# Routing in two groups with fixed 2048-row regions for each expert, and a tail summed on TensorE

## What is computed

```
x = x + align(ctx, layernorm(x))       # per batch b: ctx (77, 128)
x = x + ffn(layernorm(x))

align: D = pairwise distances (77 x 512); R = dynamic time warping cost of D
       walk back from the last cell to (0, 0); expanded[j] += ctx[i] on each cell of the path

ffn(xf), xf of shape (2048, 128), E = 8 experts, 2 chosen for each token:
       scores = sigmoid(xf @ gate_w + bias); the two largest, divided by their sum, are the weights w
       eo[e]  = gelu(xf @ up_w[e] + up_b[e]) @ down_w[e] + down_b[e]      # 128 -> 512 -> 128
       out    = 0.1 * sum over chosen e of w[e] * eo[e]  +  0.1 * (the shared expert, same form)
       out    = out / (max |out| over the row + 1e-6)
```

## Time and profile before

| | us |
|---|---|
| median of 3 runs | 290.02 |
| lowest, highest | 288.14, 290.07 |
| the profiled execution | 287.41 |
| its span (first to last instruction) | 285.7 |
| busy: PE, DVE, ACT, POOL | 161.6, 193.9, 128.6, 112.5 |

### The profile page before, as it was taken

How to read it: one execution, slowest core, us unless ns; L and a number is a source line. 1 busy time by engine, 2 the same in 40 slices (tenths; PEclk the granted TensorE clock), 3 DMA queues, 4 the chain that set the end, 5 groups by cost and what they waited for, 6 DMA issues and landing times. The chain is left out here.

```text
span 285.7 us, 5134 instructions
## 1 busy us (share of the span) xinstructions
PE 161.6 (57%) x1262; PEld 108.3 (38%) x1263; DVE 193.9 (68%) x926; ACT 128.6 (45%) x323; POOL 112.5 (39%) x210
## 2 busy tenths in 40 slices
PE   1690089991000014663478995099999999982000
PEld 0330034430000013642322331069999999972000
DVE  3843999999955816856539690058888888860590
ACT  5550049950003032295076421058888888850020
POOL 8100030000000023030477777325888888874540
PEclk9997559998555555555579999559999999999555
DMA  7013999994330000000011111222333323101922
GB/s 202 2 40 83 134 317 331 204 181 69 65 61 7 1 0 2 2 1 0 20 56 49 47 47 55 66 58 78 92 84 91 92 77 98 39 3 27 267 73 73
DMA packets 39747, 22.83 MB, mean 80 GB/s; under 512 B 14796, under 2 KB 36787, under 8 KB 39719
## 3 DMA queue, kind: packets, MB, share of 16 engines
q1 hardware_dynamic: 36824, 17.98, 27.3%
q0 software_dynamic: 2496, 4.24, 4.5%
q10 hardware_dynamic: 399, 0.28, 0.3%
HBM read 12.51 MB, written 10.89 MB: 82 GB/s over the span
## 5 line engine op out<-in xcount | busy, mean ns | idle before, releaser
L646 POOL DMA_INDIRECT expert_dram<-arena_d,result_place x46 | 47.8, 1039 | 14.7 <-issue 12.1
L793 ACT ACTIVATE arena_f<-bank,tile_bias 128x256 f32<-128x256 f32 x92 | 36.3, 474 | 3.4 <-PE bank L939 2.6
L937 PE MATMUL bank<-down_hi,arena_d 128*128 x184 | 32.8, 220 | 1.0 <-DVE arena_g L1302 1.0
L938 PE MATMUL bank<-arena_a,up_hi 128*128 128x256 f16 (+1 forms) x108 | 33.1, 307 | 0.0
L1302 DVE TENSOR_TENSOR arena_g<-arena_f,arena_d 128x512 f16<-128x512 f32 x46 | 31.8, 692 | 1.6
L939 PE MATMUL bank<-down_hi,arena_g 128*128 x184 | 32.6, 219 | 0.0
L938 PE MATMUL bank<-down_lo,arena_d 128*128 x184 | 32.6, 219 | 0.0
L605 POOL COPY met_at<-arena_b 32x3 f16 (+1 forms) x26 | 3.9, 181 | 67.6 <-DVE arena_b L1145 63.4
L1085 DVE TENSOR_TENSOR_SCAN arena_b<-arena_c,edge,arena_a 64x33 f32<-64x33 f32 x92 | 25.6, 278 | 4.7 <-DMA arena_a<-dist_dram 4.6
L884 PE MATMUL bank<-arena_b,minus_one 128*128 (+1 forms) x26 | 3.9, 185 | 43.1 <-issue 43.1
L937 PE MATMUL bank<-arena_d,up_hi 128*128 128x256 f16 x92 | 26.1, 284 | 0.5 <-DVE arena_a L1294 0.5
(11 more groups left out here) (232 smaller groups left out, 443.5 us busy)
## 6 DMA issues: line engine op xcount, KB each, us to landing
sorted_dram<-padding SPq DMA_DIRECT2D x1, 2990.0 KB, 20.6
arena_g<-sorted_dram SPq DMA_DIRECT2D x23, 130.0 KB, 2.1
arena_d<-in_L_ffn_up_w SPq DMA_DIRECT2D x6, 256.0 KB, 4.7
arena_d<-in_L_ffn_down_w SPq DMA_DIRECT2D x5, 256.0 KB, 5.2
x_sb<-in_x SPq DMA_DIRECT2D x4, 256.0 KB, 4.4
arena_b<-expert_dram SPq DMA_DIRECT2D x4, 256.0 KB, 4.0
arena_c<-expert_dram SPq DMA_DIRECT2D x4, 256.0 KB, 4.4
out<-x_sb SPq DMA_DIRECT2D x4, 256.0 KB, 2.3
```

The source lines that it names most:

```text
L646: pool.indirect_dma_start(out=expert_dram.ap(), in_=y_row[:, j % Y_SLOTS, n, :], in_offset=None, out_offset=bass.IndirectOffsetOnAxis(ap=p ...
L793: last = act.activation(hid[:, k, m, cols], banks[UP_BANK + HALVES * k + m][:, cols], ACT.Gelu, bias=bias, scale=1.0 / WSCALE)
L937: pe.matmul(o, a_hi, b_hi, start=start, stop=False)
L938: pe.matmul(o, a_hi, b_lo, start=False, stop=False)
```

## The change

Each expert gets a region of its own of 2048 rows in `sorted_dram`, which grows from 23 x 256 to 8 x 2048 + 256 = 16,640 rows. A row's place then depends on its expert and its rank alone, not on the counts of the other experts. So routing is done in two groups (`ROUTED`): batch 0 first (4 tiles), then the other 12. The places of the second group start behind the first's counts (`first_row`). GpSimd scatters batch 0's rows for both choices (8 DMAs), copies y of batch 3 for the second choice, and scatters the rest (24). VectorE's, ScalarE's and TensorE's calls are put in an order of their own for this: batch 0's logits, choice and places come before the low halves of the batches 1 to 3.

Because tiles are no longer contiguous, the first row of each of the 23 tiles is computed (`tile_row`; unused tiles point to a pad tile), and SP reads it into a register ahead of each load. The padding is written by ScalarE's queue in the loop of the weight split (at n == 2), from a source of 13 rows on each partition that lies in `x2`.

The gates are turned once, in one transpose of 128x128, and their product with the biases, laid out block by block in `bias_of_tile` (VectorE clears it, SP loads 16 small blocks during the experts), is now done in the tail. The shared expert's bias is added by ScalarE as it keeps `accT`. The shared expert uses banks 0 to 3, for which all four sums have to be copied out first (`keep_sum`).

In the tail, ScalarE's queue reads the second choices and SP's the first. TensorE sums everything in PSUM: gates times biases, `accT` times the identity (instead of the transposes), and both results times the identity. VectorE finds the peak in PSUM, ScalarE scales all four tiles of a batch, VectorE adds the residual for the batch in one operation. GpSimd has no part in it, and each batch has an output buffer of its own.

```diff
+CAPACITY = B * S
+PAD_ROW = E * CAPACITY
+FILL_ROWS = 13
+ROUTED = (0, TPB), (TPB, TILES)
...
-        sorted_dram = nc.dram_tensor("sorted_dram", (EXPERT_TILES * ET, H + 2), F32, kind="Internal")
+        sorted_dram = nc.dram_tensor("sorted_dram", (PAD_ROW + ET, H + 2), F32, kind="Internal")
...
-        S_DOWN_BANKS = 7, 5
-        S_UP_BANKS = 6, 3
+        S_DOWN_BANKS = 2, 3
+        S_UP_BANKS = 0, 1
+        GATES_BANK = 4
+        RANK_BANKS = 4, 5
...
             def load(j, k):
-                rows = sorted_dram.ap()[j * ET:(j + 1) * ET, :].rearrange("(p n) d -> p n d", n=PARTS)
-                sp.dma_start(x_row[:, k], rows).then_inc(x_row_in[k], 16)
-
+                first = sp.value_load(tile_row[0:1, j:j + 1], min_val=0, max_val=PAD_ROW)
+                sp.dma_start(x_row[:, k], sorted_dram.ap()[bass.ds(first, ET), :].rearrange("(p n) d -> p n d", n=PARTS)
+                             ).then_inc(x_row_in[k], 16)
+
+            sp.wait_ge(table_ready, 2)
             sp.wait_ge(scattered, 16 * TOP * TILES)
             for k in range(SLOTS):
                 load(k, k)
@@ -513,21 +526,18 @@
                 sp.wait_ge(xT_in_psum, j - SLOTS + 1)
                 sp.wait_ge(place_kept, j - SLOTS + 1)
                 load(j, j % SLOTS)
+                if j == SLOTS:
+                    sp.wait_ge(bias_cleared, 1)
+                if j < SLOTS + TILES:
+                    t = j - SLOTS
+                    sp.dma_start(bias_of_tile[t * E:(t + 1) * E, t * H:(t + 1) * H], down_b).then_inc(bias_in, 16)
...
+            read_results(sp, 0)
             for b in range(B):
                 sp.wait_ge(result_ready, b + 1)
-                if sum(POOL_TILES[:b + 1]):
-                    sp.wait_ge(result_by_pool, sum(POOL_TILES[:b + 1]))
-                sp.dma_start(out_tiles[b], result[:, b % 2, :, :]).then_inc(out_done[b % 2], 16)
-            for i in range(2):
-                sp.wait_ge(out_done[i], 16 * B // 2)
+                sp.dma_start(out_tiles[b], result[:, b, :, :]).then_inc(out_done, 16)
+            sp.wait_ge(out_done, 16 * B)
...
+            def second_copy(b):
+                pool.wait_ge(y2_ready, b + 1)
+                pool.tensor_copy(row_and_place2[:, batch_tiles(b), 0:H], y[:, batch_tiles(b), :]
                                  ).then_inc(second_rows, 1)
+
+            for b in range(B - 1):
+                second_copy(b)
             pool.wait_ge(zeroed, 16)
-            for k, src in enumerate((row_and_place, row_and_place2)):
-                pool.wait_ge(slots_ready, k + 1)
-                if k:
-                    pool.wait_ge(second_rows, 1 + B)
-                for t in range(TILES):
-                    pool.indirect_dma_start(
-                        out=sorted_dram.ap(), in_=src[:, t, :], in_offset=None,
-                        out_offset=bass.IndirectOffsetOnAxis(ap=slot[:, k * TILES + t:k * TILES + t + 1], axis=0)
-                    ).then_inc(scattered, 16)
-
+            for i, (t0, t1) in enumerate(ROUTED):
+                if i:
+                    second_copy(B - 1)
+                for k, src in enumerate((row_and_place, row_and_place2)):
+                    pool.wait_ge(slots_ready, TOP * i + k + 1)
+                    if k:
+                        pool.wait_ge(second_rows, 1 + (t1 // TPB if i else B - 1))
+                    for t in range(t0, t1):
+                        pool.indirect_dma_start(
+                            out=sorted_dram.ap(), in_=src[:, t, :], in_offset=None,
+                            out_offset=bass.IndirectOffsetOnAxis(ap=slot[:, k, t:t + 1], axis=0)
+                        ).then_inc(scattered, 16)
...
+            each = (PAD_ROW + ET) // P
+            pads = sorted_dram.ap().rearrange("(p j r) d -> p j (r d)", j=each // FILL_ROWS, r=FILL_ROWS)
             for n in range(2 * (E + 1) + 1):
+                if n == 2:
+                    act.wait_ge(ffn_const_ready, 1)
+                    act.dma_start(pads, padding.unsqueeze(1).to_broadcast([P, each // FILL_ROWS, FILL_ROWS * (H + 2)])
+                                  ).then_inc(zeroed, 16)
...
+            deviation(0)
+            normalise(0)
+            deviation(1)
+            normalise(1)
+            turned_high(0)
+            deviation(2)
+            deviation(3)
+            squash(0)
+            normalise(2)
+            turned_high(1)
+            normalise(3)
+            turned_high(2)
+            turned_high(3)
+            squash(1)
+            act.wait_ge(zeroed, 16)
+            for b in range(B):
...
+            for k in range(Y_SLOTS):
+                act.wait_ge(y_row_out[k], 16 * PARTS * len(range(k, EXPERT_TILES, Y_SLOTS)))
+            read_results(act, 1)
             for b in range(B):
-                if POOL_TILES[b]:
-                    act.wait_ge(tail, 2 * b + 2)
-                    if b >= 2:
-                        act.wait_ge(out_done[b % 2], 16 * (b // 2))
-                for n in range(TPB - POOL_TILES[b], TPB):
-                    act.activation(result[:, b % 2, n, :], total[:, b % 2, n, :], ACT.Copy,
-                                   scale=inv_peak[:, b, n:n + 1]).then_inc(scaled_by_act, 1)
+                act.wait_ge(tail, 2 * b + 2)
+                for n in range(TPB):
+                    last = act.activation(result[:, b, n, :], summed(b * TPB + n), ACT.Copy, scale=inv_peak[:, b, n:n + 1])
+                last.then_inc(scaled_by_act, 1)
...
+            for g in range(B):
+                add_rows(g)
+            pe.wait_ge(weights_ready, 1)
+            turn_batch(0)
+            turn_batch(1)
+            ask_gate(0)
+            turn_batch(2)
+            count_rows(0)
+            turn_batch(3)
+            for g in range(1, B):
+                ask_gate(g)
+            count_rows(1)
...
+            pe.wait_ge(gatesT_ready, 1)
+            pe.wait_ge(bias_in, 16 * TILES)
+            for b in range(B):
+                pe.matmul(banks[b][:], gatesT[:], bias_of_tile[:, b * S:(b + 1) * S], start=True, stop=False)
+                for t in group_list(b):
+                    pe.matmul(summed(t), accT[:, t * P:(t + 1) * P], ident[:], start=False, stop=False)
+            for b in range(B):
+                pe.wait_ge(by_token_in[b], 16 * TOP)
+                for k in range(TOP):
+                    mm = pe.matmul(banks[b][:], ident[:], by_token[k][:, b * S:(b + 1) * S], start=False,
+                                   stop=k == TOP - 1)
+                mm.then_inc(total_in_psum, 1)
...
+            def place_rows(i):
+                t0, t1 = ROUTED[i]
+                t, n = slice(t0, t1), t1 - t0
+                o = banks[RANK_BANKS[i]]
+                dve.wait_ge(ranks_in_psum, i + 1)
+                routed(dve.tensor_tensor_scan(running[i][:].rearrange("p e n -> p (e n)"),
+                                              carry_on[i][:].rearrange("p e n -> p (e n)"),
+                                              o[:, E * n:2 * E * n], 0.0, ALU.mult, ALU.add))
+                routed(dve.tensor_tensor(offset[i][:], o[:, 0:E * n].rearrange("p (e n) -> p e n", e=E), running[i][:],
+                                         ALU.add),
+                       lambda: dve.tensor_tensor(first_row[:, i + 1], first_row[:, i], running[i][:, :, n - 1], ALU.add
+                                                 ).then_inc(aside_ready, 1))
+                routed(dve.tensor_tensor(place[:, t].rearrange("p n e -> p e n"), each_tile(first_row[:, i], n),
+                                         offset[i][:], ALU.add))
+                routed(dve.tensor_tensor(part[:, 0, t], pick[:, 0, t], place[:, t], ALU.mult),
+                       lambda: dve.tensor_tensor(part[:, 1, t], pick[:, 1, t], place[:, t], ALU.mult
+                                                 ).then_inc(aside_ready, 1))
+                with nc.allow_low_precision(reason="one whole number and zeros"):
+                    for k in range(TOP):
+                        if k:
+                            dve.wait_ge(aside_ready, 2 * (i + 1))
+                        dve.tensor_reduce(slot[:, k, t], part[:, k, t], AX_X, ALU.add).then_inc(slots_ready, 1)
+
+            hold(0)
+            trace(0)
+            hold(1)
+            trace(1)
+            hold(2)
+            trace(2)
+            sum_stats(0)
+            hold(3)
+            spread(0)
+            trace(3)
+            sum_stats(1)
+            spread(1)
+            sum_stats(2)
+            sum_stats(3)
+            turned_low(0)
+            spread(2)
+            spread(3)
+            keep_logits(0).then_inc(logits_ready, 1)
+            choose(0)
+            place_rows(0)
+            for g in range(1, B):
+                turned_low(g)
+            for g in range(1, B):
+                ins = keep_logits(g)
+            ins.then_inc(logits_ready, 1)
+            choose(1)
+            place_rows(1)
...
             def find_peak(b):
-                dve.wait_ge(total_ready, b + 1)
```

(30 more changed lines are left out.)

312 lines of the change are left out of this document (137 added, 175 removed).

## The result

| | before | after |
|---|---|---|
| median of 4 runs each, us | 289.41 (288.14 to 290.07) | 276.99 (275.61 to 278.54) |
| profiled execution, us | 287.41 | 278.54 |
| its span | 285.7 | 276.8 |

The ratio is 0.9577, 95% interval 0.9509 to 0.9646: 12.4 us less. The prediction said 6.3 us less (283.7, range 280.0 to 290.8); the kernel came out faster than the whole range. On a second chip the same pair stood at 288.35 and 278.01, a ratio of 0.9655 (0.9597 to 0.9712), 10.3 us less.

The account below looks back on a forecast made before the run. A chain of stages bounds the kernel: routing releases 32 scatters, whose issuing sets the experts' start. Terms -7.6 + 0.7 + 0.4 - 2.8 + 3.0 = -6.3 on the median 290.02 give 283.7 us, range 280 to 290.8.

Parts of the forecast that it names:

- Tail: From the reads of the experts' results to DVE's last operation: end at 276.3 against 279.15, -2.8 us.
- First scatter: GpSimd's first scatter, released by DVE's routing chain, starts at 131.4 instead of 139.07, -7.6 us.
- Rival (d): Rest's slots late or first group's steps at full width: scatters end 2 us later, 285.7; chance 0.1.
- Rest of the scatters: Copy of batch 3 between the scatter groups, 0.61 and a restart: +0.7 us; GpSimd otherwise without a gap.
- Load: Register read and arithmetic on SP ahead of the first tile load: +0.4 us, once.
- Filling: Padding write of 8.65 MB at 0.33 MB per us lasts until 75.3, delaying weights and choices: +3.0 us.
- Rival (a): Front not hurt: queues share by bytes, the fill costs 0; 280.7 us; chance 0.2.
- the 331 GB/s of slice 6: Rate during the weights at which the prediction said DMA saturates.
- the split of the reads: Tail reads split over SP and ScalarE bring the first pair perhaps 0.4 us sooner; data set the pace.
- a pause of 1 to 3 us keeps the clock: TensorE's pause ahead of the tail's sums keeps the 2.4 GHz level; two sums of a batch take 1.8.
- Experts: First load to last y scatter stays at 79 us; later loads' register reads cost 0, at most 8 us.
- Faster by over 1%: Whole kernel below 287.1 us: first case, (a) and (d) with the edges taken off; chance 0.73.

## Why the prediction came out too small

**The term that was missing.** The largest error is one that no step mentions: 3.85 us behind the last result. The prediction counted the tail up to VectorE's end and took the rest as fixed, with both spans before it: 279.15 and 285.7. That gap of 6.55 us was never asked about. The wait of SP there, 3.9 us, with the results landed, was in the trace of before. The change takes GpSimd out of the tail altogether, and that was weighed only as arithmetic moved to TensorE. That is the step that failed: **Tail** ended its sum at DVE's last operation and put what lies behind it at nothing. What the runs showed there is GpSimd's drain, which ends 6.46 us behind GpSimd's last operation: it made up 3.85 us of the old span. One memset behind the last result put 4.1 us back, and one changed tuple took 2.6 off the kernel before. With this term the forecast would have been 279.9, just below the stated range. The other part of the miss, 3.5 us, is no mechanism: the medians lie further apart than the two profiled executions. On the second chip the saving was 10.3 us.

**First scatter, right in kind, 1.5 short.** The order of the calls was as laid out. The steps on 128x32 took 0.19 to 0.22 with 0.03 between, but for one scan of 0.52, against 0.20 and 0.03. With the front's 3.7 added, the logits were due at 128.7 and came at 127.83, the first scatter at 135.1 and came at 133.72: 0.9 of the 1.4 us was gained ahead of the logits, 0.5 behind them. Rival (d) is out: all steps but that scan cost less than their full width, and the rest's slots had 3 us to spare.

**Rest of the scatters, 0.9 short.** The copy and its restart cost 0.9 (last scatter's end 143.86 to 144.75). The other 0.7 are the 24 scatters behind it, at 1.38 us each instead of 1.34; their pauses are the same, some single ones last 1.49. That isn't shown to come from the change: the kernel before took 42.60 us for its 32 scatters in one trace and 43.68 in the other, and from start to start the last 24 take 1.31 to 1.42 us each in the twelve traces of the changed code.

**Load, 0.8 short.** The read of the register is 0.44 us on SP and 0.30 on TensorE's queue, and behind it come 0.5 us of address arithmetic and checks before the load is issued. The run with the reads moved ahead gave back 1.0.

**Filling, 0.9 too much.** The mechanism was the one described: pieces of 6,760 bytes push the weights aside, and the small write and the ships wait. Rival (a), that the queues share by bytes, is out: SP's queue had 3.13 MB to move from 42 on, which half of some 400 GB/s would have done by 58, but the last up weights, issued at 45.68, landed 25.9 us later, and ScalarE stood 14.8 us for weights. From 50 to 66 the two queues moved 890 and 891 pieces, 6.02 and 0.64 MB. (The Trainium skill, DMA: Bandwidth & Descriptors, Queues, rings and completion order, has each engine take turns between its queues by packets, not bytes; the trace agrees, with these numbers.) What was off was the speed, 0.33 MB per us taken from a window that was not full; from 46 to 70 the DMA view shows 397 to 435 GB/s. Nor are the 331 GB/s of slice 6 the ceiling that the prediction took them for. So the filling ended at 72.6 and not 75.3, and 2.1 was lost and not 3.0. That the harm follows the pieces was shown by the run of 520 bytes, where the weights came through and the ships, whose pieces are shorter still, were held up.

**Tail, right.** -2.5 for -2.8: VectorE's end 14.4 behind the first read, as written. The part of it booked for the split of the reads (0.4) wasn't there; the reason was the right one, that data set the pace. That a pause of 1 to 3 us keeps the clock held for the changed kernel (2.25 and 2.34) and not in general: at 2.43 it fell.

**Experts, right.** 79.2 us from the first load to the first read in both; the register read is covered in the loop.

**The chances.** Faster by over 1% had 0.73 and came. The range ended at 280.0, because every low case was built from terms already in the sum; none allowed for a stretch that hadn't been looked at.

## What to carry over

An engine's last operation has a price behind it: look up the closing drains and ask which engine's ends the span, before its share of a tail is weighed by arithmetic alone. A large background write has no harmless place by itself: it held up loads on other queues and, when moved, lengthened register reads more than fourfold; only beside the routing, with neither of them next to it, was no cost seen. And where a chain of matmuls waits for late data, look at the granted clock in the first of them: a pause ahead of it can cost as much as a term of the sum.

## What the runs showed of the hardware that was not expected

- GpSimd's closing drain ends 6.45 to 6.47 us behind its last operation in all fourteen traces, those of ScalarE, VectorE and TensorE 0.04 to 0.05.
- Register reads from SBUF take 0.26 to 0.29 us at rest on ScalarE, GpSimd, TensorE and VectorE, and 1.15 to 1.27 at most while 406 to 422 GB/s are written out of SBUF (at most 0.55 otherwise in this walk).
- Two queues with work for the same DMA engines went piece for piece, 890 to 891, 868 to 866 and 2140 to 2129, with pieces of 6,760 bytes against 512 and 2,048, 520 against 512 and 2,048, and 520 against 128.
- A write of 8.65 MB to DRAM in pieces of 6,760 bytes landed after 30.3 us beside the weights and 23.1 us alone (375 GB/s on average); in pieces of 520 bytes after 66.9 us.
- TensorE's clock fell to 0.50 in pauses of 2.43 to 9.56 us ahead of the tail's sums, or up to 1.0 us behind them, in five traces and held at 1.00 with pauses of 1.25 to 2.50 in seven; where it fell, the tail took 1.3 to 2.4 us longer.
- On two chips the stretch from the first load to the tail took 20% to 38% longer, with the same operations at the same durations and pauses between them. This is open.
